# Query, key and value projections from 12-bit halves: three float32r matmuls in place of one fp32 matmul

## The chip, the cores and the metric

The kernel runs on one core of one Trainium2 chip. The metric is the device time of one execution in microseconds; the time of a version is the median of its runs. Engine names below are those of the profile: PE is TensorE (matmuls; PEld its weight loads), DVE is VectorE, ACT is ScalarE, POOL is GpSimd, SP is SyncE, which here only issues transfers. A "q" behind a name is the instruction queue of that engine, where DMAs are issued.

## The reference, cut to what matters

One post-norm transformer layer in fp32: causal attention with 16 heads of 16, then a router over 16 experts of which each token takes two, beside a shared expert. The change touches the first three products only.

```python
# x: (4, 1024, 256), all weights of attention (256, 256), fp32
q = split_heads(x @ Wq + bq); k = split_heads(x @ Wk + bk); v = split_heads(x @ Wv + bv)
scores = einsum('bhqd,bhkd->bhqk', q, k) / sqrt(16), causal
out = softmax(scores) @ v, heads merged, @ Wo + bo
x = layernorm(x + out)
# router: sigmoid(x @ gate_w), top 2 of 16; experts and shared expert: silu(x @ g) * (x @ u) @ d
x = layernorm(x + shared + routed)
```

## The kernel before

The program has three blocks, and a barrier over all engines stands between each two of them.

Block one makes the projections. The 4096 tokens go through it in 8 chunks of 512 (CHUNKS), and each chunk is loaded already transposed (features on partitions) into one of two buffers xt. For a chunk, `project` on PE makes four outputs t = 0 to 3 (two halves of the features of q, two of k; 128 features by 512 tokens each, two matmuls over the 256 input features, L552), then v for four tiles of 128 tokens (128 tokens by 256 features, L564). Each q or k output is then split in three bf16 parts: ACT rounds it to the first part with the bias (`high`, L469), DVE takes the remainder (`take`, L510), ACT rounds that to the second part (`middle`, L474), POOL makes the third (`low`, L441), and SP writes the three parts to memory (`store`, L397). DVE also adds the bias of v (L517). The scores of later steps work on stacks of these parts, which SP reads back (`load_stacks`, L284, twelve DMAs for one step of four heads of one batch). In chunks 5 to 7 PE also makes the scores of the very first attention step, in pieces between the projections (`early`, 38 pieces in all), only to find each row's maximum: DVE reduces each piece (L335), and only two PSUM banks serve them, so a piece waits for the reduction of the piece two before it.

Block two is attention: 16 steps, one batch and four heads each. Block three is output projection, residual, layer norm, router, experts and second norm. It starts with the loads of x for its own chunks (`load_x`, L934) and of the gate and up weights wgu (L937); POOL adds a bias to each loaded x (`add_bias`, L958) and makes the reciprocal deviation of the chunk before (`deviation`, L963 and L965), and DVE normalises with it (`norm`, L1119).

What sets the order of work is `staggered(eng, stages, count)`: on an engine it writes turn after turn, and in turn t it runs each stage of the list for chunk t minus the stage's lag, in the order of the list. Each engine takes its instructions strictly in that order. SP's list in block one is

```python
staggered(sp, [(0, load), (1, store)], CHUNKS, turns=(0, 4))
```

so that SP issues load 0, load 1, store 0, load 2, store 1, load 3, store 2; then `load_stacks` for step 0; then load 4, store 3, load 5, store 4, load 6, store 5, load 7, store 6, `load_stacks` for step 1, and store 7. ACT, DVE and PE have one stage with lag 0 each: they go chunk by chunk.

Of the kernel before, what the change touches and what calls it, by code (L numbers as in the profile page):

```python
# [6 lines left out]
F32 = mybir.dt.float32  # L7
BF16 = mybir.dt.bfloat16
I32 = mybir.dt.int32
# [6 lines left out]
P = 128  # L16
# [19 lines left out]
KM = KS + 3  # L36

# [162 lines left out]
def build(nc, x, xT, Wq, bq, Wk, bk, Wv, bv, Wo, bo, gate_w, expert_bias, sg_w, su_w, sd_w, gu_w, down_w, out):  # L200
    with ExitStack() as ctx:
        def sb(name, shape, dt):
            return ctx.enter_context(nc.sbuf_tensor(name, shape, dt))

        def sem(name):
            return ctx.enter_context(nc.semaphore(name))
# [23 lines left out]
        wgu = sb("wgu", [P, E, DC, 2 * F], F32)  # L230
        wdn = sb("wdn", [P, E, D], F32)
# [21 lines left out]
        def piece(at, *dims):  # L253
# [19 lines left out]
        third = wgu[:, :, :, :].rearrange("p e c n -> p (e c n)")[:, 0:2 * GH * N // 2].bitcast(BF16) \  # L273
            .rearrange("p (s h t) -> p s h t", s=2, h=GH)
# [13 lines left out]
        held = ctx.enter_context(ExitStack())  # L288
# [82 lines left out]
        with ExitStack() as c1:  # L371
            xt = [piece(1024 * i, DC, CH) for i in range(2)]
            rest = [piece(2048 + 512 * t, CH) for t in range(4)]
# [76 lines left out]
            def _(act):  # L450
# [32 lines left out]
                staggered(act, [(0, split)], CHUNKS)  # L483
                act.wait_ge(big_loaded, 16 * 8)

            @blk.vector
            def _(dve):
# [4 lines left out]
                dve.wait_ge(bv_loaded, 16)  # L492

# [31 lines left out]
                staggered(dve, [(0, take)], CHUNKS, until=CHUNKS - 4)  # L525

            @blk.tensor
            def _(pe):
# [16 lines left out]
                def project(c, b, half):  # L545
                    pe.wait_ge(xt_loaded[half], 16 * b + 16)
                    for t in range(4):
                        if isinstance(c, int) and c == 0 and t % 2 == 0:
                            pe.wait_ge(wqk_loaded[t // 2], 16)
                        wait_count(pe, rest_ready[t], c)  # L550
                        for h in range(DC):
                            mm = pe.matmul(ps[:, t, :], wqk[:, t // 2, h, (t % 2) * P:(t % 2 + 1) * P],  # L552
                                           xt[half][:, h, :], start=(h == 0), stop=(h == DC - 1))
                        mm.then_inc(proj_ready[t], 1)
                        if isinstance(c, int):
                            early(c, t)
                    for i in range(2):
                        if isinstance(c, int) and c == 0 and i == 0:
                            pe.wait_ge(wv_loaded, 16)
                        wait_count(pe, v_copied[i], c)  # L560
                        for j in range(2):
                            tt = 2 * i + j
                            for h in range(DC):
                                mm = pe.matmul(ps[:, 4 + i, j * D:(j + 1) * D],  # L564
                                               xt[half][:, h, tt * P:(tt + 1) * P], wv[:, h, :],
                                               start=(h == 0), stop=(h == DC - 1))
# [231 lines left out]
        held.close()  # L798
        scores_all = sb("scores_all", [P, TILES, E], F32)
# [10 lines left out]
        with ExitStack() as c3:  # L810
# [120 lines left out]
            def _(sp):  # L931
                def load_x(c, b, r):
# [5 lines left out]
                             gu_w.rearrange("e (c p) n -> p (e c) n", p=P)).then_inc(wgu_loaded, 16)  # L938
                staggered(sp, [(0, load_x)], CHUNKS, turns=(2, CHUNKS))
# [79 lines left out]
            def _(act):  # L1019
# [69 lines left out]
                act.wait_ge(wgu_loaded, 16)  # L1089
# [243 lines left out]
            def _(pe):  # L1333
# [136 lines left out]
                pe.wait_ge(wgu_loaded, 16)  # L1470
# [35 lines left out]
```

## Time and profile before

| | |
|---|---|
| time, median of 3 runs | 1049.23 us (1042.78 to 1051.35) |
| span of the profiled execution | 975.7 us |
| outside the span (median less span) | 73.5 us |
| block one, until PE starts attention | 118.6 us |
| block two, until ACT starts block three | 488 us |
| block three | 369 us |

The profile was taken of one execution, which has no time of its own beside its span; the 73.5 us are the difference to the median and are taken as the same for both kernels. All times below are microseconds from the start of the span, unless they are marked ns. One fp32 matmul of the program shows in the trace as two MATMUL records, each with a weight load of its own.

### The profile page before, as it was taken

What the parts mean: (1) busy time and instruction counts of PE and PEld (TensorE: products, weight loads), DVE (VectorE), ACT (ScalarE), POOL (GpSimd) and SP (SyncE); (2) the same over time, 40 slices, a digit from 0 to 9 for tenths busy, and PEclk for the clock granted to TensorE, in tenths of its full rate; (3) what the DMA queues carried; (4) which work ended last, traced back from release to release, by engine and by line L of the source; (5) the groups of instructions that cost most, each with busy time, mean ns of one, the idle gap of its engine ahead of it and who ended that gap; (6) DMA issues with size and microseconds to landing.
All of it is one profiled execution on the core that took longest, in us unless ns stands there. A gap on an engine that the chain in (4) does not pass through costs nothing. (4 is left out here: it accounts for less than half of the span.)

```text
span 975.7 us, 18404 instructions
## 1 busy us (share of the span) xinstructions
PE 854.0 (88%) x5476; PEld 478.9 (49%) x5477; DVE 660.1 (68%) x1527; ACT 476.2 (49%) x686; POOL 300.0 (31%) x368
## 2 busy tenths in 40 slices
PE   7979799999999989999999997799898999999300
PEld 4635434444444434444444432687556777777200
DVE  6428688888888887888888870489892122466364
ACT  3423266656666656656666566455322444444100
POOL 3423312211112111221112211442477500464373
PEclk9979899999999999999999999889899999999755
DMA  8773855444764266425754000710126745766443
GB/s 285 193 205 131 162 67 75 100 97 59 131 85 89 36 117 118 68 38 106 130 66 57 9 2 25 235 65 23 60 103 210 232 137 152 207 207 211 157 126 95
DMA packets 82464, 113.95 MB, mean 117 GB/s; under 512 B 8945, under 2 KB 60401, under 8 KB 82417
## 3 DMA queue, kind: packets, MB, share of 16 engines
q1 hardware_dynamic: 57808, 78.01, 38.1%
q0 software_dynamic: 6720, 18.88, 5.9%
q10 hardware_dynamic: 17888, 16.41, 5.2%
q8 instruction: 31, 0.51, 0.2%
q14 instruction: 17, 0.13, 0.1%
HBM read 62.55 MB, written 50.33 MB: 116 GB/s over the span
## 5 line engine op out<-in xcount | busy, mean ns | idle before, releaser
L658 ACT ACTIVATE work<-ps 128x1024 f32<-128x1024 f32 (+3 forms) x384 | 293.8, 811 | 185.5 <-PE ps L725 185.3
L335 DVE TENSOR_REDUCE m_neg<-ps 128x1 f32<-128x512 f32 (+3 forms) x432 | 265.6, 662 | 29.2 <-PE ps L320 18.7
L629 POOL TENSOR_SCALAR_AFFINE_SELECT work<-work 128x512 f32<-128x512 f32 x128 | 81.2, 634 | 394.4 <-ACT work L658 390.0
L317 PE MATMUL ps<-stacks 96*128 96x512 bf16 (+3 forms) x528 | 151.9, 332 | 1.5 <-DVE m_neg L335 1.5
L725 PE MATMUL ps<-stacks 99*128 99x512 bf16 (+3 forms) x528 | 124.6, 329 | 6.4 <-PEq L371 4.8
L335 DVE TENSOR_REDUCE m_neg_late<-ps 128x1 f32<-128x384 f32 (+3 forms) x176 | 106.7, 636 | 27.4 <-PE ps L320 27.4
L740 PE MATMUL ps<-work,vg 128*32 128x512 f32 (+3 forms) x1056 | 112.5, 498 | 1.6 <-POOL work L629 1.6
L320 PE MATMUL ps<-mask_b,ident_b 128*128 128x128 bf16 x512 | 100.3, 223 | 0.0
L317 PEld LDWEIGHTS ps<-stacks 96*128 96x128 bf16 x528 | 50.0, 98 | 95.0 <-DVE m_neg L335 48.8
L1243 DVE TENSOR_TENSOR work<-work,ps 128x256 f32<-128x256 f32 x48 | 20.2, 421 | 106.7 <-ACT work L1062 106.7
L1421 PE MATMUL ps<-wgu,work 128*128 x384 | 91.7, 382 | 0.3 <-issue 0.3
L978 POOL DMA_INDIRECT work<-z_sorted,row_of x64 | 62.3, 974 | 85.1 <-DMA z_sorted<-work 61.7
L552 PE MATMUL ps<-work,wqk 128*128 128x512 f32 x128 | 63.5, 641 | 12.6 <-DMA work<-in_xT 7.3
L1421 PEld LDWEIGHTS ps<-wgu,work 128*128 128x128 f32 x384 | 69.8, 192 | 8.6 <-issue 1.1
L971 POOL DMA_INDIRECT y_sorted<-v_all,row_of x64 | 63.2, 988 | 31.2 <-issue 19.2
L317 PE MATMUL ps<-wgu 96*128 96x512 bf16 (+3 forms) x240 | 68.9, 329 | 0.0
L725 PEld LDWEIGHTS ps<-stacks 99*128 99x128 bf16 x528 | 44.2, 98 | 44.1 <-ACT work L658 11.1
L725 PE MATMUL ps<-wgu 99*128 99x512 bf16 (+3 forms) x240 | 57.2, 330 | 2.9 <-issue 2.9
L441 POOL TENSOR_TENSOR work<-work 128x512 bf16<-128x512 f32 x32 | 36.7, 1156 | 71.7 <-ACT work L474 71.7
L320 PEld LDWEIGHTS ps<-mask_b,ident_b 128*128 128x128 bf16 x512 | 51.1, 100 | 11.1 <-issue 3.1
L1056 ACT ACTIVATE work<-ps 128x512 f32<-128x512 f32 x48 | 28.7, 597 | 51.6 <-PE ps L1411 30.7
L740 PE MATMUL ps<-work 128*32 128x512 f32 (+3 forms) x480 | 51.2, 498 | 0.0
(143 smaller groups left out, 1098.4 us busy)
## 6 DMA issues: line engine op xcount, KB each, us to landing
stacks<-qk_parts SPq DMA_DIRECT2D x132, 128.0 KB, 6.3
qk_parts<-work SPq DMA_DIRECT2D x32, 384.0 KB, 3.0
y_sorted<-work SPq DMA_DIRECT2D x8, 1536.0 KB, 9.9
work<-y_sorted SPq DMA_DIRECT2D x48, 256.0 KB
z_sorted<-work ACTq DMA_DIRECT2D x48, 256.0 KB
wgu<-qk_parts SPq DMA_DIRECT2D x60, 128.0 KB, 6.5
work<-in_xT SPq DMA_DIRECT2D x8, 512.0 KB, 4.8
work<-in_x SPq DMA_DIRECT2D x8, 512.0 KB, 3.6
```

What stands on the lines that cost most here:

```text
L317: mm = pe.matmul(dst, qs[r][0:KS, h0 + m, qt * P:(qt + 1) * P], ks[r][0:KS, h0 + m, half * CH:half * CH + w], start=True, stop=not diag)
L320: mm = pe.matmul(dst[:, w - P:w], ident_b[:, :], mask_b[:, :], start=False, stop=True)
L335: dve.tensor_reduce(dst, ps[:, bank, 0:heads * w].rearrange("p (h k) -> p h k", h=heads), AX.X, ALU.max, negate=True).then_inc(reduced, 1)
L441: pool.tensor_tensor(parts[t][:, 2, :], rest[t], parts[t][:, 1, :], ALU.subtract).then_inc(lo_ready, 1)
L552: mm = pe.matmul(ps[:, t, :], wqk[:, t // 2, h, (t % 2) * P:(t % 2 + 1) * P], xt[half][:, h, :], start=(h == 0), stop=(h == DC - 1))
L629: pool.affine_select(out=blk_, in_=blk_, compare_op=ALU.is_ge, fill=0.0, base=0, pattern=[[0, GH], [1, P]], channel_multiplier=-1).then_in ...
L658: act.activation(probs[:, s + 2 * pair:s + 2 * pair + 2, off:CH], ps[:, SCORE_BANK + 2 * pair:SCORE_BANK + 2 * pair + 2, off:CH], ACT.Exp, ...
L725: mm = pe.matmul(ps[:, SCORE_BANK + h, off:CH], ks[r][0:KM, h, kt * P:(kt + 1) * P], qs[r][0:KM, h, qc * CH + off:(qc + 1) * CH], start=Tr ...
L740: mm = pe.matmul(ps[32 * h:32 * h + 32, OUT_BANK, off:CH], vg[r][:, kt, h, :], probs[:, s + h, off:CH], start=(kt == 0), stop=(kt == CT * ...
L971: pool.indirect_dma_start(out=y_sorted[g], out_offset=bass.IndirectOffsetOnAxis(ap=row_of[:, j, t:t + 1], axis=0), in_=y_all[:, t, :], in_ ...
L978: pool.indirect_dma_start(out=zg[u % ZSLOTS][:, j, :], out_offset=None, in_=z_sorted[u // SEC_TILES], in_offset=bass.IndirectOffsetOnAxis( ...
L1421: mm = pe.matmul(ps[:, 2 + r, 2 * F * k:2 * F * (k + 1)], ysT[r][:, h, k, :], wgu[:, bass.ds(e, 1), h, :].squeeze(1), start=(h == 0), stop ...
```

## The change

Weights and x are each split in a high half, which is rounded to float32r, and a low half, the remainder. Three float32r matmuls (high by high, high weights by low x, low weights by high x) accumulate in place of the fp32 one. The halves of the weights are made once, those of x for every chunk: ACT writes the high half (a copy with rounding), DVE subtracts. Each chunk's halves have two buffers of their own. The load of a chunk's x no longer waits until v of the chunk two before is done, but until that chunk's low half is made. To find space, the stack that lay in wgu's memory gets its own (`third`), and wgu and wdn get theirs only in block three; the load of wdn (2 MB, the down weights of the experts) moves from ACT's queue at the start of the program to SP's queue in block three, behind that of wgu.

```diff
+HALF_PRODUCTS = [(0, 0), (0, 1), (1, 0)]
...
             def _(sp):
                 def load(c, b, half):
-                    wait_count(sp, v_ready[1], c - 1)
+                    wait_count(sp, x_low[half], b)
                     sp.dma_start(xt[half], xT_v[:, :, bass.ds(c * CH, CH)]).then_inc(xt_loaded[half], 16)
...
-                act.dma_start(wdn[:, :, :], down_w.rearrange("e p n -> p e n")).then_inc(big_loaded, 16)
+                for i in range(2):
+                    act.wait_ge(wqk_loaded[i], 16)
+                    act.activation(wqk_h[0][:, i], wqk[:, i], ACT.Copy).then_inc(wqk_high[i], 1)
+                act.wait_ge(wv_loaded, 16)
+                act.activation(wv_h[0][:, :, :], wv[:, :, :], ACT.Copy).then_inc(wv_high, 1)
                 act.wait_ge(bqk_loaded, 32)
+
+                def x_high_half(c, b, half):
+                    act.wait_ge(xt_loaded[half], 16 * b + 16)
+                    wait_count(act, v_ready[1], c - 1)
+                    act.activation(x_h[half][0][:, :, :], xt[half], ACT.Copy).then_inc(x_high[half], 1)
...
-                staggered(act, [(0, split)], CHUNKS)
+                staggered(act, [(0, x_high_half), (1, split)], CHUNKS)
...
+                def x_low_half(c, b, half):
+                    dve.wait_ge(x_high[half], b + 1)
+                    dve.tensor_tensor(x_h[half][1][:, :, :], xt[half], x_h[half][0][:, :, :].bitcast(F32),
+                                      ALU.subtract).then_inc(x_low[half], 1)
...
-                staggered(dve, [(0, take)], CHUNKS, until=CHUNKS - 4)
+                staggered(dve, [(0, x_low_half), (1, take)], CHUNKS, until=CHUNKS - 4)
...
                 def project(c, b, half):
-                    pe.wait_ge(xt_loaded[half], 16 * b + 16)
+                    pe.wait_ge(x_low[half], b + 1)
...
                         for h in range(DC):
-                            mm = pe.matmul(ps[:, t, :], wqk[:, t // 2, h, (t % 2) * P:(t % 2 + 1) * P],
-                                           xt[half][:, h, :], start=(h == 0), stop=(h == DC - 1))
+                            for wp, xp in HALF_PRODUCTS:
+                                mm = pe.matmul(ps[:, t, :], wqk_h[wp][:, t // 2, h, (t % 2) * P:(t % 2 + 1) * P],
+                                               x_h[half][xp][:, h, :], start=(h == 0 and (wp, xp) == (0, 0)),
+                                               stop=(h == DC - 1 and (wp, xp) == (1, 0)))
...
                 sp.dma_start(wgu[:, :, :, :].rearrange("p e c n -> p (e c) n"),
                              gu_w.rearrange("e (c p) n -> p (e c) n", p=P)).then_inc(wgu_loaded, 16)
+                sp.dma_start(wdn[:, :, :], down_w.rearrange("e p n -> p e n")).then_inc(wgu_loaded, 16)
                 staggered(sp, [(0, load_x)], CHUNKS, turns=(2, CHUNKS))
```

Where it changes the order of instructions, two engines show it. The first place is ACT in block one, around the end of chunk 0's split; a row is one instruction with what it writes and reads, and the semaphores it waits for. Before:

```order
L474 ACTIVATE work<-work 128x512 [waits rest_ready2]
L474 ACTIVATE work<-work 128x512 [waits rest_ready3]
L469 ACTIVATE work<-ps,bqk 128x512 [waits stored0,proj_ready0]
L469 ACTIVATE work<-ps,bqk 128x512 [waits stored1,proj_ready1]
L474 ACTIVATE work<-work 128x512 [waits rest_ready0]
```

And in the changed kernel at the same place (L487 is the high half of x, L492 is `high`, L497 is `middle`):

```order
L497 ACTIVATE work<-work 128x512 [waits rest_ready2]
L497 ACTIVATE work<-work 128x512 [waits rest_ready3]
L487 ACTIVATE x_high<-work 128x1024 [waits v_ready1,xt_loaded0]
L492 ACTIVATE work<-ps,bqk 128x512 [waits stored0,proj_ready0]
L492 ACTIVATE work<-ps,bqk 128x512 [waits stored1,proj_ready1]
L497 ACTIVATE work<-work 128x512 [waits rest_ready0]
```

The high half of chunk 2 now stands between the split of chunk 0 and that of chunk 1, and waits there for the load of chunk 2.

The second place is SP at the start of block one, which the change leaves in its order. In the changed kernel:

```order
L406 DMA work<-in_xT 128x2x512 x2
L411 DMA qk_parts<-work 128x3x512 [waits lo_ready] x4
L406 DMA work<-in_xT 128x2x512 [waits x_low0]
L411 DMA qk_parts<-work 128x3x512 [waits lo_ready] x4
L406 DMA work<-in_xT 128x2x512 [waits x_low1]
```

The load of chunk 2 still stands behind the four stores of chunk 0, which wait for POOL's third parts (lo_ready).

The third place is DVE from the start of block one, in the changed kernel:

```order
L513 MEMSET stacks 3x4096 x2
L513 MEMSET third 3x4096
L519 TENSOR_TENSOR wqk_low<-wqk,wqk_high 128x512 [waits wq_high,bv_loaded,bqk_loaded]
L519 TENSOR_TENSOR wqk_low<-wqk,wqk_high 128x512 [waits wk_high]
L522 TENSOR_TENSOR wv_low<-wv,wv_high 128x512 [waits wv_high]
L527 TENSOR_TENSOR x_low<-work,x_high 128x1024 [waits x_high0]
L527 TENSOR_TENSOR x_low<-work,x_high 128x1024 [waits x_high1]
L546 SCALAR_TENSOR_TENSOR work<-ps,bqk,work 128x512 [waits hi_ready] x4
```

The three memsets, which stood ahead of the first remainder before too, now also stand ahead of the first low half, for which PE waits.

## Rows read from the trace of the kernel before

**Rows 1.** The page: its head, and the busy time of each engine

```profile
span 975.7 us, 18404 instructions
PE 854.0 (88%) x5476; PEld 478.9 (49%) x5477; DVE 660.1 (68%) x1527; ACT 476.2 (49%) x686; POOL 300.0 (31%) x368
```

**Rows 2.** Timeline of PE, block one: start, length, engine, line, what, count, [idle before]

```profile
38.95 7.03 PE L552 MATMUL ps<-work,wqk 128*128 128x512 f32 x16
45.81 3.62 PE L564 MATMUL ps<-wv,work 128*128 128x256 f32 x16
56.73 9.64 PE L552 MATMUL ps<-work,wqk 128*128 128x512 f32 x16 [7.29 <-DMA work<-in_xT]
...
118.61 1.01 PE L725 MATMUL ps<-stacks 99*128 99x512 bf16 x2 [4.84 <-PEq L371]
```

**Rows 3.** Stretches: us, busy PE PEld DVE ACT POOL, PEclk, DMA share, GB/s

```profile
56.70:69.60 12.90, 12.88 (x32) 7.11 (x33) 3.76 (x6) 4.93 (x8) 4.22 (x4) 0.80 0.60 202
69.60:84.30 14.70, 14.32 (x68) 8.38 (x67) 11.03 (x22) 4.93 (x8) 4.98 (x5) 1.00 0.52 171
```

**Rows 4.** Timeline, 0 to 30 us

```profile
5.26 9.76 PE L552 MATMUL ps<-work,wqk 128*128 128x512 f32 x16 [5.26 <-DMA wqk<-in_Wq]
...
10.27 3.47 DVE L490 MEMSET wgu<- 3x4096 bf16 x1 [0.80 <-issue]
...
26.66 2.27 POOL L441 TENSOR_TENSOR work<-work 128x512 bf16<-128x512 f32 x2 [0.56 <-ACT work L474]
...
29.37 0.54 SPq L392 DMA_DIRECT2D work<-in_xT  x1
```

**Rows 5.** Groups by line and form, 0 to 115 us: busy, mean ns, idle before

```profile
L552 PE MATMUL ps<-work,wqk 128*128 128x512 f32 x128 | 63.5, 641 | 12.6 <-DMA work<-in_xT 7.3 <-DMA wqk<-in_Wq 5.3
L441 POOL TENSOR_TENSOR work<-work 128x512 bf16<-128x512 f32 x32 | 36.7, 1156 | 71.7 <-ACT work L474 71.7
L564 PE MATMUL ps<-wv,work 128*128 128x256 f32 x128 | 29.6, 381 | 0.0
...
L510 DVE SCALAR_TENSOR_TENSOR work<-ps,bqk,work 128x512 f32<-128x512 f32 x32 | 23.8, 747 | 29.4 <-ACT work L469 29.3
L469 ACT ACTIVATE work<-ps,bqk 128x512 bf16<-128x512 f32 x32 | 22.0, 686 | 53.7 <-PE ps L552 53.6
L474 ACT ACTIVATE work<-work 128x512 bf16<-128x512 f32 x32 | 19.9, 623 | 7.8 <-DVE work L510 7.8
L335 DVE TENSOR_REDUCE m_neg<-ps 128x1 f32<-128x512 f32 x20 | 13.1, 684 | 2.8 <-PE ps L317 2.7
L517 DVE TENSOR_TENSOR v_all<-ps,bv_all 128x256 f32<-128x256 f32 x32 | 12.1, 419 | 6.8 <-PE ps L564 6.8
```

**Rows 6.** Timeline of block three: a wide ACT copy, a 512-wide DVE sum

```profile
610.76 1.05 ACT L1022 ACTIVATE work<-a_all 128x1024 f32<-128x1024 f32 x1
...
614.81 0.69 DVE L1105 TENSOR_TENSOR work<-ps,work 128x512 f32<-128x512 f32 x1 [8.35 <-PE ps L1349]
```

**Rows 7.** The eight loads of xT (source L392): their landing

```profile
DMA to landing us min/median/max: 3.5/4.8/12.1
```

**Rows 8.** Timeline of SP's queue, block one

```profile
39.83 5.74 SPq L284 DMA_DIRECT2D stacks<-qk_parts  x12
45.93 0.42 SPq L392 DMA_DIRECT2D work<-in_xT  x1
...
107.77 5.07 SPq L397 DMA_DIRECT2D qk_parts<-work  x4
```

**Rows 9.** DMA issues by line: KB, us to landing

```profile
wgu<-in_gu_w SPq DMA_DIRECT2D x1, 4096.0 KB, 17.5
```

**Rows 10.** Timeline, start of block three

```profile
607.75 0.50 SPq L937 DMA_DIRECT2D wgu<-in_gu_w  x1
...
626.81 2.37 POOL L958 TENSOR_TENSOR work<-work,bo_all 128x1024 f32<-128x1024 f32 x1 [6.00 <-DMA work<-in_x]
...
630.54 3.40 DVE L1119 TENSOR_SCALAR work<-work,moments,rstd 128x256 f32<-128x256 f32 x4 [5.15 <-POOL rstd L965]
```

More of the change, by code:

```diff
@@ L8 @@
 BF16 = mybir.dt.bfloat16
+F32R = mybir.dt.float32r
 I32 = mybir.dt.int32
@@ L229, in build @@
         wsd = sb("wsd", [P, D], F32)
-        wgu = sb("wgu", [P, E, DC, 2 * F], F32)
-        wdn = sb("wdn", [P, E, D], F32)
         ident = sb("ident", [P, P], F32)
@@ L269, in build @@
         pool_waited = sem("pool_waited")
-        third = wgu[:, :, :, :].rearrange("p e c n -> p (e c n)")[:, 0:2 * GH * N // 2].bitcast(BF16) \
-            .rearrange("p (s h t) -> p s h t", s=2, h=GH)
+        held = ctx.enter_context(ExitStack())
+        third = held.enter_context(nc.sbuf_tensor("third", [P, 2, GH, N], BF16))
         qs = [stacks[:, 0, 0], stacks[:, 1, 0], third[:, 0]]
@@ L372, in build, with halves @@
             xt = [piece(1024 * i, DC, CH) for i in range(2)]
+            def halves(name, *dims):
+                return [c1.enter_context(nc.sbuf_tensor(f"{name}_{h}", [P, *dims], F32R)) for h in ("high", "low")]
+            wqk_h = halves("wqk", 2, DC, D)
+            wv_h = halves("wv", DC, D)
+            x_h = [halves(f"x{i}", DC, CH) for i in range(2)]
+            wqk_high = [sem("wq_high"), sem("wk_high")]
+            wqk_low = [sem("wq_low"), sem("wk_low")]
+            wv_high = sem("wv_high")
+            wv_low = sem("wv_low")
+            x_high = [sem(f"x_high{i}") for i in range(2)]
+            x_low = [sem(f"x_low{i}") for i in range(2)]
             rest = [piece(2048 + 512 * t, CH) for t in range(4)]
@@ L563, in project @@
                             for h in range(DC):
-                                mm = pe.matmul(ps[:, 4 + i, j * D:(j + 1) * D],
-                                               xt[half][:, h, tt * P:(tt + 1) * P], wv[:, h, :],
-                                               start=(h == 0), stop=(h == DC - 1))
+                                for wp, xp in HALF_PRODUCTS:
+                                    mm = pe.matmul(ps[:, 4 + i, j * D:(j + 1) * D],
+                                                   x_h[half][xp][:, h, tt * P:(tt + 1) * P], wv_h[wp][:, h, :],
+                                                   start=(h == 0 and (wp, xp) == (0, 0)),
+                                                   stop=(h == DC - 1 and (wp, xp) == (1, 0)))
                         mm.then_inc(v_ready[i], 1)
@@ L798, in build @@
         held.close()
+        wgu = sb("wgu", [P, E, DC, 2 * F], F32)
+        wdn = sb("wdn", [P, E, D], F32)
         scores_all = sb("scores_all", [P, TILES, E], F32)
@@ L1088, in _ @@
                 staggered(act, [(0, gate)], CHUNKS, turns=(2, CHUNKS))
-                act.wait_ge(wgu_loaded, 16)
+                act.wait_ge(wgu_loaded, 32)
                 for g in range(SECTIONS):
@@ L1469, in _ @@
                 pe.wait_ge(shared_done, 2 * CHUNKS)
-                pe.wait_ge(wgu_loaded, 16)
+                pe.wait_ge(wgu_loaded, 32)
                 pe.wait_ge(blocks_ready, SECTIONS)
```

14 lines of the change are left out of this document (10 added, 4 removed).

## The prediction

> **What bounds the kernel now.** I read the page first: PE is busy 88% of a span of 975.7 us, DVE 68% [rows 1]. The change touches block one, which ends when PE starts attention at 118.61 [rows 2], and the first loads of block three, so only these are worked out.
>
> In block one PE's timeline shows chunks back to back: the 16 records of q and k start at 38.95, those of v at 45.81 [rows 2], so a q or k record takes 6.86 / 16 = 0.43 us. A v record has half the columns, 0.21 us, and a chunk takes 6.86 + 3.45 = 10.3 us. Then PE stands idle 7.29 us for the load of chunk 4 and starts at 56.73, with its first 16 records in 9.64 us, 2.8 more than above [rows 2]; the granted clock of that stretch was 0.80, and 1.00 in the next [rows 3]: behind the idle time part of the chunk ran at the lower level, 1.2 GHz. The idle time has its cause on SP: the load of chunk 4 is issued at 45.93, behind twelve DMAs that began at 39.83 [rows 8], and lands 10.8 later. In chunks 5 to 7 PE is busy 14.32 of 14.70 us and DVE 11.03 [rows 3]; a chunk there takes some 14.7. Groups by line give what one chunk costs the other engines [rows 5]: ACT 4 x (0.69 + 0.62) = 5.2, POOL 4 x 1.16 = 4.6, DVE 4 x 0.75 + 4 x 0.42 = 4.7, and 8.7 more for about 13 reductions in chunks 5 to 7. So PE is the bound, and nobody else is near it.
>
> **What the change takes from PE.** A record of an fp32 matmul makes two passes over its columns. If a float32r matmul is one pass, it costs 0.21 us for 512 columns and 0.11 for 256. A chunk then has 24 of either: 24 x 0.21 + 24 x 0.11 = 7.7 us, 2.6 less than 10.3. No row shows float32r; the ends are one pass and an fp32 record's price (0.43 and 0.21, a chunk of 15.5 us). I take one pass, since three products at two passes each would make more passes than fp32's four.
>
> A page of the Trainium skill says the same from its side: "FP8 and Floating Point Precision", TensorE Precision Notes, gives true fp32 four passes, and reduced precision fp32 read as FP22. By that rule alone the time would fall by 8 x 2.6 = 21 us, which is the first rival below.
>
> **Start.** PE began at 5.26 [rows 4]; now it needs the low halves, and DVE makes them behind its memsets, the last of which ends at 10.27 + 3.47 = 13.7 [rows 4]. A DVE sum of 512 elements takes 0.69 [rows 6] and one of 256 takes 0.42 [rows 5], which is 1.05 ns for an element more, so 1024 elements take 1.23. Three weight halves and x of chunk 0: 13.7 + 3 x 0.69 + 1.23 = 17.0. ACT's part (three copies of 0.62, two of 1.05 [rows 5, 6]) is done behind these memsets. PE starts 11.8 us later. Its first 16 records took 9.76 before [rows 4], where 6.86 is the later pace, and I carry these 2.9, some 2.6 of it ahead of the last of q and k: chunk 0's are ready at 17.0 + 24 x 0.21 + 2.6 = 24.7.
>
> **The loop that the new order closes.** This is the main term. In turn t ACT now runs the high half of x(t) and only then the split of chunk t-1, and DVE the low half and then `take` of t-1. But SP issues load t behind the stores of chunk t-2. So: x(t) lands, split t-1, stores t-1, load t+1, x(t+1) lands. One chunk for each round trip. Before, load t+1 had to be there only for PE's chunk t+1, and the split of chunk t went on without it: two chunks for a trip.
>
> Its length from the landing of x(t), with q and k of t-1 ready: ACT's copy 1.05; DVE's low half until 2.3; the first remainder until 3.1 (0.75); the first `middle` until 3.7; ACT then alternates, 0.69 and 0.62, the last `high` until 5.6, the last remainder 6.4, the last `middle` 7.0. POOL follows every 1.16 from 3.7: 4 x 1.16 = 4.6, end at 8.3. The load is issued 0.44 behind POOL's end (26.66 + 2.27 = 28.93, load at 29.37 [rows 4]) and lands 4.8 later, the median [rows 7]. Sum 13.6 us a chunk. Against this PE has 7.7 of work and waits; where it cools in the gaps, 10.5.
>
> The landing can be 3.5, the least of that row, or some 6, since the stores now follow each other every 1.16 instead of every 1.7: 12.3 to 14.8 a round. Here a page of the Trainium skill has a rule: "DMA: Bandwidth & Descriptors" (its opening section on the two cost components) gives 2.0 us plus the bytes over 436 GB/s, which for 512 KB is 3.2 us, an estimate from that page. The row says 4.8 at the median and never below 3.5; by the page the sum would be 5 x 1.6 = 8 us less, near 1083.
>
> **The sum of block one**, by the landing X(t) of x(t):
> - X(2): q and k of chunk 0 at 24.7; behind them the last low part at 28.3 (0.69, 0.75, 0.62 and 1.16, with 0.4 of queueing), issue 0.44, landing 4.8: 33.5.
> - X(3): 33.5 + 13.6 = 47.1.
> - X(4): 8.3 until chunk 2's last part, 0.6 until the twelve stack DMAs, 6.1 for these (39.83 to 45.93 [rows 8]), 10.8 to landing: 47.1 + 25.8 = 72.9.
> - X(5), X(6): 86.5 and 100.1.
> - X(7): `take` of chunk 5 now has nine reductions of 0.68 between its four remainders [rows 5]: 2.3 + 6.1 + 3.0 = 11.4, then 0.62 + 1.16 + 0.44 + 4.8; 1 more for PE, which is cold after the wait and has pieces to make: 19.5, so 119.6.
> - End: DVE does its low half (2.3), the rest of chunk 6 (8.7 + 4.7 + 1.1 of small steps), and chunk 7 up to its last remainder (9.1): 25.9; last part at 27.7. Before, attention began 118.61 - 112.84 = 5.8 behind the last store's issue [rows 2, 8], whose own length is 0.4: X(7) + 34 = 153.6.
>
> Block one ends at 153.6 against 118.6: **+35 us**. PE's 21 us are all inside waits.
>
> **Block three.** wgu's load is issued at 607.75 and takes 17.5 for 4 MB [rows 9, 10], until 625.3. x of chunk 2 stands behind it on SP's queue; POOL waited 6.00 us for it, until 626.81, and DVE 5.15 for POOL, until 630.54 [rows 10]. wdn's 2 MB now go between them. Their price lies between 0 (should the transfers share the engines so that x passes) and half of 17.5, 8.7. Without the first 1 MB of x, which goes ahead and leaves 14.8 us for wgu, half is 7.4, and I take 7.3. Nothing absorbs it: the deviation of chunk 1 stands behind that bias on POOL, and chunk by chunk norm, residual and statistics hang on each other. **+7 us**. That wdn is gone from the start of the program frees transfers beside chunk 0, where PE waited for none: nothing gained. The waits for wgu_loaded come 60 us and more after the load: nothing. The other moves of memory add no instruction.
>
> **Forecast**: span 975.7 + 35 + 7 = 1018; with 73.5 around it, 1091.
>
> **Rivals.**
> 1. *PE's passes decide, the rest hides.* For it speaks that PE is the bound now [rows 3]. It needs the x loads to be early, and no delay at the start beyond ACT's copies (about +5 instead of +11.8). Then 8 chunks save 2.6 each, 21, less 5 and nothing for wdn: 1033. The rows on SP's order and the trip speak against it. It decides only if the round trip falls under 7.7. 3%.
> 2. *The loop is there but shorter than PE and DVE need.* Chunk 4 then starts at 63.9 (start +11.8, three chunks at 2.6 less, the same stack loads), early chunks take DVE's 14.2, block one ends at 120.5: +2, and wdn +7: 1058. 7%.
> 3. *float32r at the price of an fp32 record.* PE's chunk of 15.5 exceeds the loop by 1.9 in five chunks, and in chunks 5 to 7 adds some 3 each: +17, 1108. 8%.
>
> **Chances and range.** My case has 82%: with landing 3.5 to 6 (six trips, -7 to +7), wdn 0 to 8.7 (-7 to +2) and 3 for the clock, 1077 to 1103. To take in part of the others the range is 1070 to 1108. A change of 1% (10 us) is about what this measurement can tell. Faster by over 1%: 3%; within: 7%; slower: 90%.
>
> **What would show it.** In block one of the new profile: ACT waits about 5 us per chunk for xT before its 1024-wide copy; PE waits for DVE's low half and its clock falls in between; chunks start some 13.6 apart; PE's first matmul is at 17; attention begins near 154; float32r matmuls start 0.21 apart. In block three POOL's third bias waits 13 us instead of 6. Wrong would be chunks 8 to 10 apart (rival 2), or spacings of 0.43 (rival 3).

## The result, and the profile after

The changed kernel takes **1087.86 us** at the median of 4 runs (1087.58 to 1092.78), the kernel before on the same chip 1048.1 (1042.78 to 1051.35). The ratio is 1.0391, with a 95% interval of 1.0348 to 1.0434: 40 us slower. The forecast was 1091.

The head of the page and the busy time of each engine, as in [rows 1]:

```profile
span 1085.8 us, 18681 instructions
...
PE 863.2 (79%) x5604; PEld 503.1 (46%) x5605; DVE 670.8 (62%) x1538; ACT 484.4 (45%) x697; POOL 299.0 (28%) x368
```

This execution took 1087.78 us, 2 more than its span. The profiled execution of before had a span of 975.7 [rows 1], which I had set against a median of 1049. The two spans are 110 us apart, the two medians 40: 70 us of it have nothing to do with the change, and are taken up at the end. So I compare landmarks instead of spans.

Timeline of PE in block one: the start, the float32r matmuls of one chunk, and the first matmul of attention, as [rows 2, 4]:

```profile
16.87 0.80 PE L589 MATMUL ps<-x_high,wqk_high 128*128 128x512 f32 x1 [16.87 <-DVE x_low L527]
...
23.06 0.40 PE L589 MATMUL ps<-x_high,wqk_high 128*128 128x512 f32 x1
23.29 0.40 PE L589 MATMUL ps<-x_low,wqk_high 128*128 128x512 f32 x1
...
25.25 0.28 PE L603 MATMUL ps<-wv_high,x_low 128*128 128x256 f32 x1
25.37 0.28 PE L603 MATMUL ps<-wv_low,x_high 128*128 128x256 f32 x1
...
28.01 0.40 PE L589 MATMUL ps<-x_high,wqk_high 128*128 128x512 f32 x1
...
36.41 0.47 PE L589 MATMUL ps<-x_high,wqk_high 128*128 128x512 f32 x1
...
152.44 1.01 PE L765 MATMUL ps<-stacks 99*128 99x512 bf16 x2 [7.18 <-PEq L372]
```

The second number of a single record is its own length, which overlaps the next; the pace is the distance of the starts, 0.23 us for 512 columns and 0.12 for 256. A chunk with no wait goes from 28.01 to 36.41, 8.4 us against 10.3 before. Attention starts at 152.44, where it started at 118.61 [rows 2]: 33.8 later.

Timeline of ACT, line L487: the high half of x for chunks 2 to 7. The bracket is the idle time ahead of it and what ended that:

```profile
33.28 1.06 ACT L487 ACTIVATE x_high<-work 128x1024 fp32r<-128x1024 f32 x1 [5.80 <-DMA work<-in_xT]
46.08 1.06 ACT L487 ACTIVATE x_high<-work 128x1024 fp32r<-128x1024 f32 x1 [6.03 <-DMA work<-in_xT]
72.22 1.06 ACT L487 ACTIVATE x_high<-work 128x1024 fp32r<-128x1024 f32 x1 [19.38 <-DMA work<-in_xT]
86.51 1.06 ACT L487 ACTIVATE x_high<-work 128x1024 fp32r<-128x1024 f32 x1 [7.53 <-DMA work<-in_xT]
100.06 1.06 ACT L487 ACTIVATE x_high<-work 128x1024 fp32r<-128x1024 f32 x1 [6.79 <-DMA work<-in_xT]
118.51 1.06 ACT L487 ACTIVATE x_high<-work 128x1024 fp32r<-128x1024 f32 x1 [5.75 <-DMA work<-in_xT]
```

These six starts are 12.8, 26.1, 14.3, 13.6 and 18.5 apart. One round of them on the other queues, between the first row and the second (SPq is SP's queue):

```profile
34.37 1.23 DVE L527 TENSOR_TENSOR x_low<-work,x_high 128x1024 fp32r<-128x1024 f32 x1 [5.41 <-ACT x_high L487]
...
37.00 4.55 POOL L455 TENSOR_TENSOR work<-work 128x512 bf16<-128x512 f32 x4 [8.09 <-ACT work L497]
...
38.20 3.75 SPq L411 DMA_DIRECT2D qk_parts<-work  x4
41.99 0.53 SPq L406 DMA_DIRECT2D work<-in_xT  x1
...
75.94 4.54 POOL L455 TENSOR_TENSOR work<-work 128x512 bf16<-128x512 f32 x4 [21.61 <-ACT work L497]
...
81.61 0.40 SPq L406 DMA_DIRECT2D work<-in_xT  x1
```

x lands at 33.3; DVE does the low half; POOL's last part of the chunk ahead ends at 41.55; its stores are issued until 41.95; only then is the next load issued, and 4.1 us later ACT starts on it. The round is 8.27 to POOL's end, 0.44 to the issue and 4.09 to ACT. The last two rows are of the round from 72.22: 8.26, 1.13 and 4.90. The waits of block one (0 to 165 us: in total, times, longest) say the same from the waiting engines' side:

```profile
ACT x_high L487 <- DMA work<-in_xT: 51.3, 6, 19.4
DVE x_low L527 <- ACT x_high L487: 49.6, 6, 19.8
...
PE ps L589 <- DVE work L546: 23.4, 3, 16.0
```

Stretches of block one, columns as in [rows 3]: us; busy PE, PEld, DVE, ACT, POOL; PEclk, DMA share, GB/s. The first is one round:

```profile
36.40:49.50 13.10, 8.88 (x50) 7.71 (x50) 5.67 (x10) 5.97 (x10) 4.55 (x4) 1.00 0.48 160
49.50:76.00 26.50, 10.55 (x50) 8.87 (x49) 5.58 (x10) 6.02 (x11) 4.60 (x5) 0.70 0.77 139
76.00:90.00 14.00, 10.75 (x50) 8.99 (x49) 5.22 (x9) 5.37 (x9) 4.48 (x4) 0.84 0.46 152
```

Nobody is near full in a round: PE has 8.9 of 13.1 and 10.8 of 14 us, the second at a lower clock, DVE, ACT and POOL some 5 or 6 each. Behind its long wait PE's granted clock was 0.70 in the second stretch and 0.84 in the third, against 1.00 in the first.

Block three starts at 641.22, before at 606.76, 34.5 later. Its start, as [rows 10]:

```profile
642.76 11.23 SPq L981 DMA_DIRECT2D wdn<-in_down_w  x1
...
668.03 2.34 POOL L1001 TENSOR_TENSOR work<-work,bo_all 128x1024 f32<-128x1024 f32 x1 [11.66 <-DMA work<-in_x]
...
671.73 3.39 DVE L1162 TENSOR_SCALAR work<-work,moments,rstd 128x256 f32<-128x256 f32 x4 [10.77 <-POOL rstd L1008]
```

The waits are 5.7 and 5.6 longer than in [rows 10], and both rows stand 41.2 later than theirs there: 6.7 of it come in block three. SP's timelines show the way of the delay: wdn's own issue holds the queue 11.2 us, so that x of chunk 2 is issued 13.2 us behind the start of the block and no longer 10.7, and POOL has it 13.7 us after its issue instead of 9.4.

### The profile page after: what moved, and what is told of

Its sections match the earlier page's. It is cut to its first block and busy times, and to the rows that moved or that the text cites. A ratio compares the mean times of both kernels' runs of the same rounds, so it can differ in the third digit from the quotient of the medians.

```text
span 1085.8 us, 18681 instructions
## 1 busy us (share of the span) xinstructions
PE 863.2 (79%) x5604; PEld 503.1 (46%) x5605; DVE 670.8 (62%) x1538; ACT 484.4 (45%) x697; POOL 299.0 (28%) x368
## 5 line engine op out<-in xcount | busy, mean ns | idle before, releaser
L318 PE MATMUL ps<-stacks 96*128 96x512 bf16 (+3 forms) x528 | 154.1, 336 | 12.3 <-DVE m_neg L336 12.3
L1464 PE MATMUL ps<-wgu,work 128*128 x384 | 100.3, 408 | 10.9 <-ACT work L1099 7.9
L1464 PEld LDWEIGHTS ps<-wgu,work 128*128 128x128 f32 x384 | 75.0, 206 | 22.0 <-issue 12.5
L318 PE MATMUL ps<-third 96*128 96x512 bf16 (+3 forms) x240 | 68.8, 329 | 0.0
L589 PE MATMUL ps<-x_high,wqk_high 128*128 128x512 f32 x64 | 31.3, 489 | 40.3 <-DVE work L546 23.4
L765 PE MATMUL ps<-third 99*128 99x512 bf16 (+3 forms) x240 | 57.8, 333 | 3.1 <-issue 3.1
L1480 PE MATMUL ps<-wdn,work 128*128 x192 | 52.0, 395 | 2.0 <-DVE work L1292 1.8
```

Of the source, the lines that this page charges most:

```text
L318: mm = pe.matmul(dst, qs[r][0:KS, h0 + m, qt * P:(qt + 1) * P], ks[r][0:KS, h0 + m, half * CH:half * CH + w], start=True, stop=not diag)
L765: mm = pe.matmul(ps[:, SCORE_BANK + h, off:CH], ks[r][0:KM, h, kt * P:(kt + 1) * P], qs[r][0:KM, h, qc * CH + off:(qc + 1) * CH], start=Tr ...
L1464: mm = pe.matmul(ps[:, 2 + r, 2 * F * k:2 * F * (k + 1)], ysT[r][:, h, k, :], wgu[:, bass.ds(e, 1), h, :].squeeze(1), start=(h == 0), stop ...
L1480: mm = pe.matmul(ps[:, 6 + r, D * k:D * (k + 1)], hxT[r][:, k, :], wdn[:, bass.ds(e, 1), :].squeeze(1), start=True, stop=True)
```

## The experiments

Each kernel is timed against the kernel before on its own chip, and the ratio is to that. For experiments 7, 10 and 11 that was one of 1045.67 us, near the 1048.1 of the comparison above; for all others one of 976 to 979. "Block one ends" is the start of attention.

**1. The kernel before once more**, unchanged.

> The kernel before, unchanged, for a second profile. In the profile of the changed kernel block one ends 33.8 us later and block three starts 34.5 later, as forecast, but the span is 110 us longer while the median time is only 40 longer; between 750 and 840 us all engines stand still for stretches that no engine ends. Theory: these stretches occur in executions of either kernel, and the first profile of the kernel before happened to have few, so that its 73.5 us outside the span were really such time. Then this profile shows a span within 5 us of its own time, near 1045, with attention starting near 118 and a block three of some 430 to 440 us. Rival: they come with the change (the later wdn load, the memory layout); then the span is again near 976 beside a time of 1048.

Measured 978.13 us (975.31 to 984.47), against 979.06 for the same kernel: 0.9995 [0.9973, 1.0017]. Its profiled execution, by core, and the end of block one:

```profile
core 0: 979.7 us, clock 0.940
```

```profile
118.64 1.01 PE L725 MATMUL ps<-stacks 99*128 99x512 bf16 x2 [4.52 <-PEq L371]
```

That execution took 981.73, 2.0 more than its span. The times I had written down did not come, because this chip needs 979 for the kernel, not 1049. But the question is answered: nothing to speak of lies outside the span, and my 73.5 was no such thing.

**2. Loads ahead of the stores.** Only the order on SP is altered: the stores of a chunk stand one turn later, behind the next load.

```diff
-                staggered(sp, [(0, load), (1, store)], CHUNKS, turns=(0, 4))
+                staggered(sp, [(0, load), (2, store)], CHUNKS, turns=(0, 4))
...
-                staggered(sp, [(0, load), (1, store)], CHUNKS, turns=(4, 8))
+                staggered(sp, [(0, load), (2, store)], CHUNKS, turns=(4, 8))
+                store(CHUNKS - 2, B - 1, 0)
```

> The changed kernel with one thing different: SP writes its stores one turn later (lag 2), so that the load of x for chunk t+1 is issued ahead of the stores of chunk t-1. Theory (the round trip split, store, load, high half is the loop that sets the pace): the six waits of ACT for xT (51.3 us in sum) nearly vanish, except perhaps for chunk 4 behind the stack DMAs, chunks 1 to 3 start 8 to 10 us apart, and block one ends at 118 to 124 instead of 152.4; the time falls by some 30 us, to 1055 to 1062. Rival (the chunks are slow because of the longer chain of halves through ACT and DVE and the cold clock, whatever the load does): block one ends above 140, the time falls by under 12 us.

Measured 984.36 (982.83 to 994.59), 1.0061 [1.0032, 1.0089]. The changed kernel itself takes 1016.59 in its own comparison (experiment 5, before 978.79): 32 us come back. In the timeline and in the waits:

```profile
56.01 1.06 ACT L488 ACTIVATE x_high<-work 128x1024 fp32r<-128x1024 f32 x1 [12.25 <-DMA work<-in_xT]
...
119.14 1.01 PE L766 MATMUL ps<-stacks 99*128 99x512 bf16 x2 [6.63 <-PEq L372]
```

```profile
ACT x_high L488 <- DMA work<-in_xT: 12.2, 1, 12.2
```

ACT waits once for x, for chunk 4 behind the stack DMAs, and no longer six times; block one ends at 119.1 instead of 152.0. The loop is real, and it is nearly the whole of block one's loss.

**3. wdn behind the x loads.**

```diff
-                sp.dma_start(wdn[:, :, :], down_w.rearrange("e p n -> p e n")).then_inc(wgu_loaded, 16)
                 staggered(sp, [(0, load_x)], CHUNKS, turns=(2, CHUNKS))
+                sp.dma_start(wdn[:, :, :], down_w.rearrange("e p n -> p e n")).then_inc(wgu_loaded, 16)
```

> The changed kernel with one thing different: the load of wdn stands on SP's queue behind all loads of x in block three instead of between wgu and x of chunk 2. Theory: POOL's wait for x of chunk 2 goes from 11.7 back to 6 us, its third bias starts some 20 us after the start of block three instead of 26.8, and the time falls by 5 to 7 us, to 1081 to 1083. Rival (the transfers share the engines, or later slack takes the delay up): the third bias moves, but the time stays within 2 us of 1088.

Measured 1014.79 (1012.43 to 1017.76), 1.0354 [1.0319, 1.0389]. POOL's third bias:

```profile
666.70 2.37 POOL L1001 TENSOR_TENSOR work<-work,bo_all 128x1024 f32<-128x1024 f32 x1 [5.02 <-DMA work<-in_x]
```

The wait is back at 5.0 us, and block three took 368.5 in this profile against 375.3 in experiment 5's. The median moved by only 1.8 where 5 to 7 were expected, by the ratios it is 4.7, and the two intervals overlap; block two took 497 us in this execution. The place is confirmed here, the price by experiment 4.

**4. wdn moved in the kernel before, and nothing else.**

```diff
-                act.dma_start(wdn[:, :, :], down_w.rearrange("e p n -> p e n")).then_inc(big_loaded, 16)
...
                 sp.dma_start(wgu[:, :, :, :].rearrange("p e c n -> p (e c) n"),
                              gu_w.rearrange("e (c p) n -> p (e c) n", p=P)).then_inc(wgu_loaded, 16)
+                sp.dma_start(wdn[:, :, :], down_w.rearrange("e p n -> p e n")).then_inc(wgu_loaded, 16)
```

> The kernel before, fp32, with one part of the change alone: the load of wdn leaves ACT's queue at the start and stands on SP's queue in block three, behind wgu and ahead of x of chunk 2. Its memory stays where it was. Theory: block one is untouched (attention starts at 118 to 119), POOL's wait for x of chunk 2 goes from 6 to 12 us, block three is 6 to 7 us longer, and the time is 0.6 to 0.7% above the kernel before on the same chip. Rival: block three takes the delay up later, or the start gains what it loses there: within 0.2%.

Measured 984.51 (981.49 to 987.1) against 976.43: 1.0070 [1.0047, 1.0094], 6.9 us at the ratio. Block one ends at 119.09, near the 118.6 of before: that wdn was gone from the start gained nothing there. The third bias waits as in the changed kernel:

```profile
635.69 2.34 POOL L958 TENSOR_TENSOR work<-work,bo_all 128x1024 f32<-128x1024 f32 x1 [11.63 <-DMA work<-in_x]
```

**5. The changed kernel once more**, unchanged, on a chip with a kernel before of 978.79.

> The changed kernel, unchanged, on the chip of the experiments, where the kernel before took 979.1 (a median of 15 runs) with a span of 979.7 and nothing outside. Theory: the 70 us by which the first comparison's times lay above this belong to that chip and to both kernels, and the change is worth what the forecast's two terms say, 34 for block one and 6 to 7 for block three: 1017 to 1022, the wait of POOL for x of chunk 2 near 12 us, block one until 150 to 153. Rival: part of the stretches without work in the first profile comes with the change; then it is over 1030.

Measured 1016.59 (1014.71 to 1024.88), 1.0402 [1.0344, 1.046]:

```profile
151.99 1.01 PE L765 MATMUL ps<-stacks 99*128 99x512 bf16 x2 [5.97 <-PEq L372]
...
667.29 2.34 POOL L1001 TENSOR_TENSOR work<-work,bo_all 128x1024 f32<-128x1024 f32 x1 [12.41 <-DMA work<-in_x]
```

The same landmarks, the same 38 to 40 us over the kernel before, at a level 71 us lower. Whatever makes that level, the change doesn't meet it.

**6. PE's passes made dear again.** In the changed kernel one plain fp32 matmul of the high halves takes the place of three float32r ones, for q, k and v; the products with a low half are left out.

```diff
-HALF_PRODUCTS = [(0, 0), (0, 1), (1, 0)]
+HALF_PRODUCTS = [(0, 0)]
...
-                                mm = pe.matmul(ps[:, t, :], wqk_h[wp][:, t // 2, h, (t % 2) * P:(t % 2 + 1) * P],
+                                mm = pe.matmul(ps[:, t, :], wqk_h[wp][:, t // 2, h, (t % 2) * P:(t % 2 + 1) * P].bitcast(F32),
```

> The changed kernel with everything kept (halves made, order, waits), but for the product: one plain fp32 matmul of the two high halves in place of the three float32r ones. It leaves the low halves out of the product, so its result has lost precision; its time shows what PE's passes are worth. Four passes instead of three, 2.6 us more per chunk. Theory (the loop sets the pace, PE waits inside it): block one ends within 3 us of 152.4, at most 5 later for the last chunks, and the time within 5 us of 1088. Rival (PE's passes decide): 8 x 2.6 = 21 us more, about 1108.

Measured 1019.19 (1016.1 to 1020.88), 1.0413 [1.0382, 1.0444], beside 1.0402 for the changed kernel.

```profile
151.89 1.01 PE L765 MATMUL ps<-stacks 99*128 99x512 bf16 x2 [4.76 <-PEq L372]
```

ACT waits 50.6 us for x in six waits, as before the edit, and block one ends at the same place. What float32r saves on PE, some 2 us in each of eight chunks, is worth nothing in this order.

**7. PE's work cut to a third.** The changed kernel with one float32r product; both products with a low half are left out. One run, in the group with a kernel before of 1045.67.

```diff
-HALF_PRODUCTS = [(0, 0), (0, 1), (1, 0)]
+HALF_PRODUCTS = [(0, 0)]
```

> The changed kernel in its own order, with one float32r matmul (high by high) instead of three; it leaves both low products out. PE's work in block one falls to a third, by 5 us a chunk. Theory (the round trip sets the pace): block one ends at 147 to 152 instead of 152.0, since only chunk 0 and the last chunks have PE on the path; time 1011 to 1017. Rival (PE decides): 8 x 5 = 40 us less, below 985.

Measured 1081.78, 36 over the kernel before of its group; the changed kernel was 40 over its own.

```profile
142.59 1.01 PE L765 MATMUL ps<-stacks 99*128 99x512 bf16 x2 [8.13 <-PEq L372]
```

The high halves start at 29.57, 42.34, 67.79, 80.88, 93.95 and 110.62: the rounds are still 12.8 and 13.1, and ACT waits 49.3 us in six waits, though PE has a third of its work. The end comes 9.9 earlier than in the changed kernel's first profile, outside the 147 to 152 that I had expected: 3.7 ahead of the first round, which does begin with PE's q and k, 2.4 in the rounds to chunk 6, 1.8 in the one with chunk 5's reductions (16.7 for 18.5), and 2.0 behind the last x. The loop sets the end, with a small share of PE in it: PE lost some 45 us of work (8 chunks of 16 x 0.23 + 16 x 0.12), and 9.9 of it showed. The time is of a single run, and block two took 495 us in it.

**8. Everything undone that costs**: experiments 2 and 3 together, and the three stack memsets of DVE moved from the start behind chunks 0, 1 and 2.

```diff
-                for r in range(STACKS):
-                    dve.memset(ks[r][KS:KM], 1.0).then_inc(ones_ready, 1)
                 dve.wait_ge(bqk_loaded, 32)
...
-                staggered(dve, [(0, x_low_half), (1, take)], CHUNKS, until=CHUNKS - 4)
+                staggered(dve, [(0, x_low_half), (1, take)], CHUNKS, turns=(0, 2))
+                for r in range(STACKS):
+                    dve.memset(ks[r][KS:KM], 1.0).then_inc(ones_ready, 1)
+                    staggered(dve, [(0, x_low_half), (1, take)], CHUNKS, turns=(r + 2, r + 3))
+                staggered(dve, [(0, x_low_half), (1, take)], CHUNKS, turns=(STACKS + 2, CHUNKS + 1), until=CHUNKS - 4)
```

> The changed kernel with three things different: the x loads one turn ahead of the stores, the wdn load behind the x loads of block three, and DVE's three memsets spread behind chunks 0, 1 and 2 instead of ahead of the first low halves. Theory: PE starts at 11 to 12 (behind ACT's table load, three weight copies and the copy of x) instead of 16.9, the memsets cost nothing later, block one ends at 113 to 116, and block three gives back 6: 971 to 976 where the kernel before has 979. Rival: the wait of chunk 4 behind the stack DMAs takes up what the earlier start gives, block one still ends near 119, and the time is 978 or more.

Measured 978.09 (975.49 to 984.03), 0.9998 [0.9973, 1.0023].

```profile
12.93 0.79 PE L592 MATMUL ps<-x_high,wqk_high 128*128 128x512 f32 x1 [12.93 <-DVE x_low L526]
...
117.06 1.01 PE L768 MATMUL ps<-stacks 99*128 99x512 bf16 x2 [6.69 <-PEq L372]
```

The start came 4 us earlier and block one ended only 2 earlier than in experiment 2. The wait for chunk 4 took up the earlier start: ACT's copy of that chunk began at 55.90 against 56.01 there. Where the 2 us at the end come from is not shown. With all three prices paid back, the change is worth nothing measurable. The expected 971 to 976 did not come; the rival's 978 did.

**9. Chunk 4's load ahead of the stack DMAs**, on top of experiment 8.

```diff
-                staggered(sp, [(0, load), (2, store)], CHUNKS, turns=(0, 4))
+                staggered(sp, [(0, load), (2, store)], CHUNKS, turns=(0, 5))
...
-                staggered(sp, [(0, load), (2, store)], CHUNKS, turns=(4, 8))
+                staggered(sp, [(0, load), (2, store)], CHUNKS, turns=(5, 8))
```

> As the kernel with x loads ahead, wdn late and memsets spread, and with one thing more: the load of chunk 4 and the stores of chunk 2 stand ahead of the twelve stack DMAs. With the loads ahead alone ACT still waited 12.2 us for xT once, in chunk 4. Theory: that wait vanishes and chunk 4's half of it is not given back, so block one ends 7 to 11 us earlier than without this and the time is 962 to 969, clearly below the kernel before. Rival: the stacks then come late for the early pieces of chunk 5 and DVE, which is busy 13.6 of 14 us there, holds the end where it was: under 3 us gained.

Measured 978.64 (977.93 to 984.19), 1.0000 [0.9982, 1.0019]. Timeline, then the stretch of a late chunk:

```profile
63.26 1.06 ACT L488 ACTIVATE x_high<-work 128x1024 fp32r<-128x1024 f32 x1 [7.85 <-DMA work<-in_xT]
...
117.08 1.01 PE L768 MATMUL ps<-stacks 99*128 99x512 bf16 x2 [6.47 <-PEq L372]
```

```profile
84.00:98.00 14.00, 12.95 (x80) 9.49 (x79) 13.65 (x28) 6.06 (x9) 4.65 (x4) 1.00 0.33 112
```

Nothing was gained where 962 to 969 had been expected. The wait has gone one chunk on, to chunk 5, and in this stretch DVE is busy 13.65 of 14 us. The same stretch of the kernel before:

```profile
84.00:98.00 14.00, 13.39 (x59) 7.31 (x58) 11.73 (x23) 4.93 (x8) 4.14 (x4) 1.00 0.38 123
```

Of DVE's 1.9 us more, 1.2 are the low half. That this made DVE the bound of the late chunks is an argument from busy times, PE having 12.95; experiment 10 puts it to the test.

**10. Low half of x on POOL from chunk 2 on**, on top of experiment 9; against a kernel before of 1045.67.

```diff
+                def x_low_later(c, b, half):
...
+                    pool.tensor_tensor(x_h[half][1][:, :, :], xt[half], x_h[half][0][:, :, :].bitcast(F32),
+                                       ALU.subtract).then_inc(x_low[half], 1)
+
+                staggered(pool, [(0, x_low_later), (1, low)], CHUNKS)
```

> The kernel with all four edits of order and with one thing more: from chunk 2 on POOL makes the low half of x instead of DVE. Theory: DVE is the bound of chunks 5 to 7 (13.3 to 13.7 of 14.0 us), its low half costs 1.2 of them a chunk and POOL has the room (4.6 to 7.5 of 14), so block one ends 2 to 4 us earlier, at 113 to 115, and the time is 974 to 976. Rival: POOL needs 2.3 us for it, ahead of the third parts of the chunk before, and hands the delay to the stores and to PE's start of the chunk: nothing gained or up to 3 us lost, 978 to 981.

Measured 1043.89 (1037.84 to 1051.06), 0.9965 [0.993, 0.9999].

```profile
114.65 1.01 PE L777 MATMUL ps<-stacks 99*128 99x512 bf16 x2 [6.11 <-PEq L372]
```

```profile
84.00:98.00 14.00, 13.22 (x82) 9.64 (x81) 12.69 (x23) 5.35 (x9) 6.05 (x5) 1.00 0.38 119
```

Block one is 2.4 us shorter than in experiment 9 and 4.0 shorter than in the kernel before. DVE has a little room again. Its low halves were in the way, for 2.4 us of block one, although POOL needs 2.4 us for each where DVE needed 1.2; in the time the gain is at the edge of what can be told from none.

**11. fp32 in that order**: experiment 9's order with one plain fp32 matmul of the high halves, the products with a low half left out (the edit of experiment 6); same group as experiment 10.

> The kernel with all four edits of order (loads ahead, wdn late, memsets spread, chunk 4's load first), but with one plain fp32 matmul of the two high halves in place of the three float32r ones, as in the experiment of the same kind before. It leaves the low halves out of the product. It asks what the three passes are worth once nothing else waits for x. Theory: in chunks 5 to 7 DVE is busy 13.3 to 13.7 of 14.0 us and PE 12.0 to 13.0, so PE with 2.6 us more a chunk just becomes the bound, as in the kernel before; block one ends at 119 to 122 instead of 117.1, time 980 to 984. Rival (PE's passes are still hidden whole): block one within 1 us of 117.1, 978 to 979.5.

Measured 1051.95 (1047.14 to 1059.7), 1.0076 [1.0049, 1.0104].

```profile
121.33 1.01 PE L768 MATMUL ps<-stacks 99*128 99x512 bf16 x2 [4.65 <-PEq L372]
```

```profile
84.00:98.00 14.00, 13.40 (x58) 7.03 (x57) 12.37 (x25) 5.44 (x9) 3.54 (x4) 1.00 0.28 95
```

Block one ends at 121.3 with fp32 and at 117.1 with float32r. Out of the loop, float32r is worth 4 us of block one against fp32 that still makes the halves. The times differ by more, 0.76% by the ratios of experiments 9 and 11, which is 7 to 8 us, where the expected 980 to 984 stood for 1 to 5 more than 979; block one shows 4 of them, and where the rest lies is open. What the halves themselves cost no run isolates.

**12. The kernel before with chunk 4's load ahead of the stack DMAs.**

```diff
                 staggered(sp, [(0, load), (1, store)], CHUNKS, turns=(0, 4))
+                load(4, 2, 0)
                 for t in range(4):
                     sp.wait_ge(stored[t], 16 * HALVES)
                 load_stacks(sp, 0, 0)
-                staggered(sp, [(0, load), (1, store)], CHUNKS, turns=(4, 8))
+                store(3, 1, 1)
+                staggered(sp, [(0, load), (1, store)], CHUNKS, turns=(5, 8))
```

> The kernel before, still fp32, with one thing different: the load of chunk 4 is issued ahead of the twelve stack DMAs. It tells how much of a better version's gain is float32r's and how much the order of the loads. Theory: PE's wait of 6.8 to 7.3 us for that load vanishes with the cold chunk behind it (2.8), chunks 4 to 7 follow at once, and the time falls by 8 to 10 us, to 969 to 971. If float32r is worth something on top, the kernel with all four edits lies below that; if DVE bounds chunks 5 to 7 in both, they are within 4 us. Rival: the stores of chunk 3 behind the stack DMAs hold up ACT, which needs their buffers, and the gain is under 4.

Measured 973.33 (970.69 to 976.05), **0.9941** [0.9921, 0.9962], the lowest ratio of the study and the only one clearly below 1 (the interval of experiment 10 ends at 0.9999).

```profile
115.54 1.01 PE L727 MATMUL ps<-stacks 99*128 99x512 bf16 x2 [5.24 <-PEq L371]
```

```profile
ACT work L471 <- DMA qk_parts<-work: 11.0, 2, 10.5
...
PE ps L554 <- DMA work<-in_xT: 3.0, 1, 3.0
```

PE goes from chunk 3 to chunk 4 with no wait, where it stood 7.29 us [rows 2], and waits 3.0 us for x of chunk 5 instead: as in experiment 9, part of the wait has gone one chunk on. It gave 5.5 of the 8 to 10 us hoped for. ACT waits 10.5 us, ahead of chunk 4's first parts, for the stores of chunk 3's parts, which free their buffer and stand behind the twelve stack DMAs. That was the rival's mechanism, though the gain is above the rival's 4.

## Why the prediction was right

**The loop**, its main term, held by place and by size. The landmarks, forecast and measured (X is the start of ACT's copy of that chunk):

| | forecast | measured |
|---|---|---|
| PE's first matmul | 17.0 | 16.87 |
| X(2), X(3) | 33.5, 47.1 | 33.28, 46.08 |
| X(4) | 72.9 | 72.22 |
| X(5), X(6) | 86.5, 100.1 | 86.51, 100.06 |
| X(7) | 119.6 | 118.51 |
| start of attention | 153.6 | 152.44 |

Experiment 2 opens the loop by order alone and gets 32 us back; experiments 6 and 7 make PE's work dearer and cheaper and leave ACT's six waits at 50.6 and 49.3 us in sum, against 51.3. The first rival (PE's passes decide) would have needed block one to move by what PE gained or lost, some 15 us later in experiment 6 and some 45 earlier in experiment 7; it moved by less than 1 and by 9.9. The second (a loop shorter than PE and DVE need) would have had no waits for x.

Two landmarks behind the last x agree with the forecast in their sum and not in their parts. The last low part ended 26.0 us after X(7), forecast 27.7, and attention began 7.9 behind that, forecast 6.3. That they add up to 33.9 for 34 is luck.

**Block three**: +7 forecast, 6.7 in the two timelines, 6.9 with wdn moved alone. The third bias waited 11.66, forecast 13: 5.7 of the price are on that wait, and 1 was lost ahead of it. The size that I took, some half of wgu's time for half its bytes, was right to within the runs, and experiment 4 shows that the move of wdn is the cause. But I had put all of it on shared transfers: 2.5 us came from the later issue of x, behind wdn's own, and 4.3 from its longer landing.

**PE's saving is inside waits**: held, by experiment 6. But its size was off. I had half the price of an fp32 record, 0.21 and 0.11 us; float32r matmuls start 0.23 and 0.12 apart. A chunk took 8.4 instead of 7.7, and the saving was 1.9 instead of 2.6. The third rival (0.43 a matmul) is refuted by the same rows. A matmul of 512 columns costs 0.23 against 0.86 for the two records of fp32. The Trainium skill's page "FP8 and Floating Point Precision", TensorE Precision Notes, gives fp32 four passes; the ratio here is 3.7, so the trace nearly agrees, and yet none of it reached the time.

**The landing** of xT was 4.1 us at the median (3.7 to 10.8) instead of 4.8. The page "DMA: Bandwidth & Descriptors" of the Trainium skill (its opening section on the two cost components) gives 2.0 us plus the bytes over 436 GB/s, so 3.2 for 512 KB, an estimate; its fit is for transfers issued from GpSimd, and these are issued from SP. No load of xT in any run was so fast (3.4 at least). The split, forecast at 8.3, took 8.27 and 8.26. The first round was 12.8 and not 13.6, by the landing alone. In the two rounds behind the stack DMAs the load was issued 1.13 behind POOL's end instead of 0.44, and the round from 72.22 had a landing of 4.9: 14.3. These small errors of opposite sign met near the forecast, which is luck. No run tells why the issue came later there.

**What was wrong** is "with 73.5 around it". The step took the span of one execution and the median of others for two parts of one thing, and called the difference time outside the span. Experiment 1 shows 2 us outside. The sum went by differences, so that the error stood on both sides and fell out; the span of 1018 that it gave for the changed kernel is what a chip with the lower level shows (1015.9, experiment 5), and not the chip of the comparison (1085.8).

Two sums of the rivals don't come out. From the terms named for rival 2 chunk 4 starts at 60.7, or at 63.0 with the copies of its halves, and not at 63.9; and rival 3's terms, 5 x 1.9 and 3 x 3, make 18.5 and not 17. Neither changes what the runs decide.

## What to carry to other kernels

A stage added to a pipeline that is written out engine by engine can close a loop that no single line shows. Follow one buffer through all queues in program order, and for each wait ask whether the awaited transfer is issued behind something that needs the work queued behind this wait; if so, price the round trip and compare it with the busiest engine's chunk. Move a large load only together with the queue it leaves and the queue it joins: the 2 MB cost nothing where they were and 6.9 us in front of the loads that another engine was waiting for. And a faster form on the bound engine pays only what the engines that feed it leave of it: here the passes gave 4 us of block one on PE (experiment 11), the low halves on DVE took 2.4 (experiment 10), and the whole came out at no gain (experiments 8 and 9).

## What the runs showed of the hardware

**The pace of float32r.** At the full granted clock (2.4 GHz), matmuls of 512 columns start 0.23 us apart and those of 256 columns 0.12; an fp32 record of the kernel before took 0.43 and 0.21 [rows 2], and there are two to a matmul. A matmul of 512 columns is so 0.23 against 0.86.

**A level 70 us higher in some comparisons.** The kernel before took 1048 and 1046 us in two groups and 976 to 979 in the others, each steady to within about 1%. In the high one the extra time is in block three: it took 439 to 445 us in the four profiled executions at that level (the changed kernel and experiments 7, 10 and 11) and 368 to 376 in all others, the profile behind [rows 1] among them. There engines stand still and the trace names no engine that they wait for; its "remote" is an event from outside the core's engines and known queues. Timeline of ACT, changed kernel, 1087.78 us:

```profile
834.75 0.38 ACT L1105 ACTIVATE work<-ps 128x256 f32<-128x256 f32 x1 [17.60 <-remote]
```

The stretch from 740 to 840 us, changed kernel, first in that execution and then in experiment 5's:

```profile
740.00:840.00 100.00, 49.38 (x149) 29.96 (x148) 35.15 (x107) 10.36 (x16) 57.28 (x59) 0.74 0.27 93
```

```profile
740.00:840.00 100.00, 92.89 (x411) 68.02 (x411) 44.29 (x127) 33.68 (x59) 56.26 (x58) 0.96 0.54 167
```

PE does 149 matmuls instead of 411 in these 100 us, and the DMA engines are half as busy. The changed kernel's block one and two were the same at both levels to within 1 us; its block three took 444.6 us at the high level and 375.3 at the low. I made no experiment on its cause, and it stays open; the ratios of the change, 1.0391 and 1.0402, are the same at both levels.

**Block two** took 487 to 491 us in ten profiled executions and 495 to 498 in four others (experiments 2, 3, 7 and 11), of kernels that do the same work there. One profile's span is therefore no better than 1%, and what is under that has to come from the repeated runs.
